# ScalarE's order within a chunk: the Sign pass ahead of that chunk's adjacency loads

## The reference

```
# layer 1
h = item_feat @ W_item.T + b_item
b = x @ W_user.T + b_user
x = layernorm(x + relu(adj @ h + b))
# layer 2
Wh = x @ W;  e = leaky_relu(Wh @ a[:128] + (Wh @ a[128:]).T, 0.2)
p  = softmax(where(adj > 0, e, -9e15), axis=1)
x  = layernorm(x + elu(p @ Wh))
```

## Time and profile before

| | us |
|---|---|
| median of 3 runs | 3150.01 |
| lowest and highest | 3139.74, 3197.87 |
| the profiled execution | 3156.98 |
| its span, first to last instruction | 3155.2 |
| span in which `adj` is loaded | 0 to about 1640 |

### The profile page before, as it was taken

One profiled execution on the slowest core, in us unless ns is written; L12 is line 12 of the kernel. 1 busy time (PEld: TensorE's weight loads), 2 busy tenths in 40 slices (PEclk: granted clock), 3 DMA queues, 4 the chain that ended last, 5 costly groups with the idle time before them and its releaser, 6 DMA issues.

```text
span 3155.2 us, 50455 instructions
## 1 busy us (share of the span) xinstructions
PE 2947.8 (93%) x16484; PEld 2121.8 (67%) x16484; DVE 2646.8 (84%) x3522; ACT 861.7 (27%) x506; POOL 246.6 (8%) x186
## 2 busy tenths in 40 slices
PE   8999998888997889899997999999999999999998
PEld 5444443343443334344477999999999999999995
DVE  5888876676775677677779999999999999999995
ACT  3555444344443344444441100000000000000000
POOL 0000000000000000000003111112111111111120
PEclk9999999999999999899998999999999999999999
DMA  9999999999999999999971000000000000000000
GB/s 268 314 302 300 286 272 247 233 250 246 277 271 217 230 263 270 237 275 271 264 176 60 12 19 21 19 15 15 18 15 15 15 15 15 15 23 15 15 7 9
DMA packets 498749, 457.98 MB, mean 145 GB/s; under 512 B 39744, under 2 KB 490992, under 8 KB 498544
## 3 DMA queue, kind: packets, MB, share of 16 engines
q1 hardware_dynamic: 248352, 233.87, 30.2%
q10 hardware_dynamic: 250320, 223.28, 29.1%
HBM read 433.81 MB, written 23.22 MB: 145 GB/s over the span
## 4 chain that ended last, share of the span: by engine, by line
PE 60%; DMA 18%; ACTq 8%; DVE 8%; issue 4%; ACT 1%; DVEq 0%; SPq 0%
PE bank L631 42%; DMA area<-in_adj_dram 18%; PE bank L573 17%; ACTq L979 7%; DVE area L691 3%; DVE area_s L844 2%; DVE unpacked L902 1%; PE bank L598 0%; ACTq L1017 0%; DMA area_x<-in_L_gnn_item_feat_dram 0%; ACT area_m L1011 0%; PE bank L510 0%; PE bank L552 0%; ACT area L1123 0%; DVEq L924 0%
## 5 line engine op out<-in xcount | busy, mean ns | idle before, releaser
L631 PE MATMUL bank<-area_h,area_s 128*128 (+2 forms) x12482 | 1443.6, 277 | 47.2 <-DVE area_s L844 47.2
L573 PE MATMUL bank<-area,area_h 128*128 128x512 f32 (+1 forms) x3160 | 1396.9, 600 | 86.0 <-DVE area L691 85.5
L631 PEld LDWEIGHTS bank<-area_h,area_s 128*128 128x128 f32 (+1 forms) x12482 | 1405.9, 191 | 83.6 <-issue 72.0
L691 DVE STREAM_TRANSPOSE area<-area 128x2048 f32<-128x2048 f32 (+3 forms) x400 | 894.1, 2235 | 376.9 <-DMA area<-in_adj_dram 270.3
L844 DVE SCALAR_TENSOR_TENSOR area_s<-area,c_col,unpacked 128x512 f32<-128x512 uint8 (+2 forms) x1580 | 1170.3, 801 | 37.9 <-PE bank L631 26.2
L573 PEld LDWEIGHTS bank<-area,area_h 128*128 128x128 f32 x3160 | 609.8, 196 | 817.2 <-issue 719.5
L1011 ACT ACTIVATE area_m<-area 128x4096 uint8<-128x4096 f32 (+1 forms) x200 | 700.1, 3501 | 853.5 <-issue 582.4
L1171 ACT ACTIVATE std_o<-mv,eps_col 128x4 f32<-128x4 f32 (+1 forms) x20 | 6.0, 298 | 929.2 <-DVE mv L869 929.2
L902 DVE TENSOR_TENSOR unpacked<-area,bit_of 128x1024 uint32<-128x1024 uint32 (+1 forms) x200 | 246.1, 1231 | 0.0
L736 DVE SCALAR_TENSOR_TENSOR packing<-area_m 128x512 uint32<-128x512 uint32 (+1 forms) x200 | 134.0, 670 | 38.6 <-ACT area_m L1011 38.5
L458 POOL COPY area_x<-area_s 128x512 f32 (+1 forms) x19 | 11.7, 613 | 1603.8 <-ACT area_s L1058 1603.8
(11 more groups left out here) (102 smaller groups left out, 674.3 us busy)
## 6 DMA issues: line engine op xcount, KB each, us to landing
area<-in_adj_dram SPq DMA_DIRECT2D x702, 256.0 KB, 8.3
area<-in_adj_dram ACTq DMA_DIRECT2D x702, 256.0 KB, 10.5
area<-in_adj_dram SPq DMA_DIRECT2D x78, 196.0 KB, 6.9
area<-in_adj_dram ACTq DMA_DIRECT2D x78, 196.0 KB, 8.4
mask_scratch<-packed ACTq DMA_DIRECT2D x38, 320.0 KB, 13.1
area<-mask_scratch SPq DMA_DIRECT2D x19, 640.0 KB, 3.9
x_scratch<-area_s ACTq DMA_DIRECT2D x20, 256.0 KB, 14.6
area<-x_scratch SPq DMA_DIRECT2D x20, 256.0 KB, 2.8
```

Of the source, the lines that this page charges most:

```text
L573: mm = nc.tensor.matmul(acc[par][:, 0:width], h[:, c * SPC + s, :], adj_t[:, c % 2, s * width:(s + 1) * width], start=(c == 0 and s == 0), ...
L631: mm = nc.tensor.matmul(bank[0:m, (t % 2) * DEN:(t % 2 + 1) * DEN], prob[:, slot, t * P:t * P + m], right, start=start and t % 2 == 0, sto ...
L691: nc.vector.transpose(dst, src).then_inc(half_turned, 1)
```

## The change

Two calls change places in ScalarE's loop over chunks of layer 1:

```
                 for c in range(NC):
+                    mask_chunk(k, c, width)
                     loads_ahead(k, c, nxt)
-                    mask_chunk(k, c, width)
                     if not first:
```

## The result

The changed kernel takes **3265.76 us** (median of 3 runs, 3250.89 to 3269.03) against 3150.01 us: by the comparison on the same chip a ratio of **1.037**, 95% interval 1.029 to 1.046, so slower. Some executions of one kernel come out over a per cent slower than its fastest, and the ratios leave those out. The profiled execution has a span of 3267.2 us, 112.0 us more than before.

What follows compares the result with a forecast made beforehand. The prediction took the loop of five slots as the bound for three quarters of layer 1: 3157 + 111 + 5 - 15 = 3258 us, forecast as 3250 since the runs' median is 7 us below the profiled one; range 3190 to 3310.

Steps and rivals of the forecast that it cites:

- Layer 2 untouched: The calls that change places exist only in layer 1, so layer 2, from about 1640 us on, keeps its time.
- The early pair is held back by a half's period: ScalarE's early loads in layer 1 wait one half longer: 4.2 us from 400 to 1600, 3.6 us from 100 to 400.
- the loads don't wait for the Sign pass to run: ScalarE's sequencer hands the pass on and issues loads meanwhile; of its 3.6 us they pay about nothing.
- Rival 4: Not as described: loads wait for the Sign pass to end, each delay grows by 3.6 us; 3550 us, chance 0.02.
- The price from 400 to 1600: Layer 1's five-slot loop: 163 halves without slack, 33 turns at 3.4 us each, 111 us, between 0 and 194.
- the two queues' balance: ScalarE's loads fall behind SyncE's in each chunk, so one queue works alone more; inside the range, not in the sum.
- The first stretch: Layer 1 from 100 to 400 us, bound by TensorE: slack covers most of the hold, 5 us charged, 0 to 30.
- The Sign pass's gain: VectorE's waits on the Sign pass, 38.1 us, should vanish as it starts earlier: 0 to -38 us, taken as -15.
- Rival 1: ScalarE's queue is nearly always backlogged from 400 us on, so later issue costs nothing: 3135 us, chance 0.24.
- Rival 2: The late Sign pass upset layer 1's pace; with it first the fast state lasts: 3050 us, chance 0.12.
- Rival 3: The queues' balance sets layer 1's rate; fast stretches lost, slow ones slower: 3406 us, half of it 3320; chance 0.12.
- the mark of my price: VectorE's wait on `adj` rising from 262 us towards 370 would show the price right; unchanged, that loads were absorbed.

Runs made afterwards that it cites:

- e3: The changed kernel with SyncE's early pair held back by one half as well, so both queues hold theirs; ratio 0.984 to the kernel before.
- e7: The kernel before with the early pairs of both queues held back by one half, Sign pass last as before; ratio 0.975.
- e6: The kernel before with four slots in place of five, so every load of both queues goes out one half later; ratio 0.964 (3017 us).
- e1: The changed kernel with the Sign pass between ScalarE's early and late pair of loads, so neither pair is held back; ratio 1.026 to the kernel before.
- e5: The kernel before with the quarters of a half dealt crosswise, so each queue writes both sides of the partitions; ratio 1.050.
- e12: The kernel before with four slots and the scores stored as one row in place of 512 single words; ratio 0.955, 3002 us.
- e4: The kernel before with only SyncE's early pair held back by one half, ScalarE's order untouched; ratio 1.013.

## Why the prediction was right, and where its reasons were not

- **The number**: 3250 forecast, 3266 measured, well inside 3190 to 3310. That it is so close is luck: the terms were +111, +5 and -15 us, and what was measured is about +65 from 400 to 1600, +28 from 100 to 400, no gain by the Sign pass, and some 19 us outside both stretches.
- **Layer 2 untouched**: right, both ends of it moved by the same 112 us.
- **The early pair is held back by a half's period, the loads don't wait for the Sign pass to run, all four go out in a burst**: right, 4.2 us at 831.78, with the pass at 831.57. Rival 4 falls with it.
- **The price from 400 to 1600, 111 us, as a delay paid once in each turn of slots without slack**: this is the step that failed. The size was off too (about 65 us in this stretch), and so was the delay in it, 3.4 us per half: counted to the end of a pair's issue, ScalarE's loads go out a mean 1.3 us later, because the issues themselves got shorter. Above all, e3, e7 and e6 delay more loads and are faster. A wait of VectorE on an `adj` DMA doesn't say that the slots are too few; it says that the later queue's part was missing. What the runs put in its place is the step of the two queues: with SyncE held as well, the change's 1.037 becomes 0.984. I had this as "the two queues' balance", rested on the earlier trace rows, and left it out of the sum. How the step costs is only half known: about half of the loss goes through the one-sided stretches, the rest is open.
- **The first stretch, 5 us (0 to 30)**: mis-sized; 28 us. VectorE's wait there went from 6.3 us to 57.2. I expected over 60 only if the high rate was lost; that is what began.
- **The Sign pass's gain, -15 us**: the waits vanished as I said, and nothing was gained; e1 gains nothing from the earlier pass, and e3 beside e7 suggests a cost near 1%, some 30 us. Why an earlier pass costs isn't settled: in e1 the lag is 3.8 us in place of 3.2 and ScalarE's loads land 13.3 us after their issue in place of 12.2, but what in the pass does that no run here tells apart.
- **Rival 1** (absorbed by the backlog), and with it the rule of the Trainium skill that queues only save issue time (page "DMA: Bandwidth & Descriptors", section "Issuing engines are not separate DMA queues"): refuted for these kernels, where each queue writes its own side of the partitions: 224 GB/s in a stretch with one queue at work and 357 in one with both, 211 and 261 over all stretches of the kernel before. Where both write both sides (e5), the bytes per second didn't depend on it, 245 against 246 GB/s, as the rule has it. The backlog itself was real in part, as the 1.3 us in place of 3.4 say.
- **Rival 2** (the Sign pass upset the pace): wrong about the cause, and right that the high rate can be kept; e7 and e12 keep it.
- **Rival 3** (balance): the right mechanism, at less than half of its size: 116 us in place of 256. Half of it would have been 3278 us, not the 3320 that I wrote, and so inside my own range.

VectorE's wait on `adj` rose to 379 us, which I had written as the mark of my price (towards 370). It fits both mechanisms, so it was no test of them. A mark that would have told them apart is the bytes by queue in short stretches.

## What to carry to other kernels

When two DMA queues fill the two parts of one buffer, look at whether their loads go out at the same moments; here a delay on one of them cost, and the same delay on both gained. The lag between the queues' issues for the same buffer is easy to count from a trace, and the five-slot kernels with each side to one queue stand nearly in its order: 0.3 us at ratio 0.975, 0.7 at 0.984, 3.2 at 1, 4.4 at 1.037; e4, with 0.4 us and 1.013, is the exception. Before adding buffers to a loop that waits for DMAs, try one fewer: here ScalarE's issues took a median of 1256 ns against SyncE's 317, its loads went out 3.2 us behind, and one slot less cured both. And a change that seems to free an engine is to be costed by what it does to the order in which that engine issues DMAs.

## What the runs showed of the hardware that I had not expected

- The share of time in which the DMA engines are busy is 1.09 at 357 GB/s and 1.14 at 219 and 224. It can't be read as nearness to a limit.
- One queue nearly alone moved 219 and 224 GB/s when it wrote one side of the partitions and 239 when it wrote both; two queues with a side each moved 357, two dealt crosswise 314 in a good stretch.
- Behind a DMA of 512 single words, 2 KB in all, both queues together fell to 116 GB/s for 8 us, and behind each of the first 18 such stores to between 70 and 165. With one row in its place the kernel is 2.2% faster.
- Issuing a DMA on ScalarE took a median of 1256 ns with five slots in flight and 383 ns with four, for the same transfer.
